# Eight experts' weights prepared beside the QKV projection, low-half stores moved to SyncE's queue, and ring registers kept for the down products

## The chip, the cores and the metric

The kernel runs on one core of a Trainium2 chip. The core has five engines with queues of their own: TensorE (PE), VectorE (DVE), ScalarE (ACT), GpSimd (POOL) and SyncE (SP). They share 16 DMA engines. A transfer is issued from the queue of one engine; in the profile those of SP are in q1 (hardware_dynamic) and those of POOL in q0 (software_dynamic). The metric is the device time of one execution in microseconds. Times differ by about 0.2% between executions of one kernel (2583.82 to 2589.56 us in three runs of the kernel before).

## The reference, cut to what matters

Two transformer layers over x of 2 x 1024 tokens of width 512, all float32. The change touches the first two of their four parts:

```
x = x + attention(layernorm(x))      # 16 heads of width 32, causal, per batch of 1024 tokens
x = x + experts(layernorm(x))        # 32 experts, top 8 per token, inner width 192
...
# attention
q, k, v = x @ Wq + bq, x @ Wk + bk, x @ Wv + bv        # per head
y = softmax(mask(q @ k.T) * scale) @ v
out = concat(y) @ Wo + bo
# experts
w, e = softmax(top_k(x @ gate_w.T, 8)), indices
h = silu(x @ w_gate[e].T) * (x @ w_up[e].T) * w
out = sum over e of h @ w_down[e].T
```

## The kernel before, in words

Matrix products are made of float32 values split in a high half (rounded to the form that PE reads fast, called fp32r in the profile) and a low half (the rest); a product is then the sum of high x high, low x high and high x low. So each operand has to be split first, and each split costs a copy for the high half and a subtraction for the low one.

**The QKV stage** (`norm_and_project`). x is 16 tiles of 128 tokens. Each is normalized by DVE, turned over by PE (`turn`), and its halves x_hi and x_lo are kept in SBUF for all tokens. The projection of queries and keys has 32 steps (`STEPS`: 4 groups of 512 tokens x 8 columns of 128 outputs), each of 12 matmuls into one of four PSUM buffers; a step for the values (`values`, 12 matmuls) follows every second of them. For every q/k step n, ACT writes the high half (`high_qk`, tile qk_hi), DVE the low half (`low_qk`, tile qk_lo), and both go to DRAM, 256 KB each, since attention wants them in another layout. There are three buffers of each (`BUFS = 3`): step n+3 waits until the stores of step n have landed. The high half is stored from SP's queue (L312), the low half from POOL's (L326). `home` gives the place of a store in DRAM: 4 heads x 32 rows x 512 tokens, so 128 rows of 2 KB.

The order on PE is written out: `UNITS` are the q/k and value steps. The turning of the 12 later tiles stands between the first 12 units, one after each.

**The attention stage** (`attend`). 16 heads, two per loop body. While PE, ACT and DVE work on a head, POOL splits expert weights that the later experts stage needs: per head two experts, each with a load of gate/up weights (768 KB), a cast and a subtraction, a store of both halves (1536 KB), then the same for the down weights (512 KB in, 768 KB out). POOL also copies each head's values into v_pair (L577), and PE's `output` waits for that. The q and k rows of the next heads are loaded by SP (L651, L655) when the columns of a head are done; the head's result is stored by SP too (L667, L668).

**The experts stage**. 160 blocks of 128 rows, 16 to a loop body on PE. Each step of PE turns the x of the next block, makes the down product of the block two steps back (`down`, L1453), turns h of the one before and makes the gate/up product of its own block (`up`, L1433). The weights lie in a ring in SBUF, and `ring_place` (L1424) loads the ring place of a block from a table into a register of PE's sequencer: once for `up` and again, two steps later, for `down` of the same block.

Each stage ends when all engines have passed it, the stores' landing included: SP waits for hi_stored and POOL for lo_stored at the end of the QKV stage.

Of the kernel before, what the change touches and what calls it, by code (L numbers as in the profile page):

```python
# [12 lines left out]
P = 128  # L13
# [212 lines left out]
def attention(nc, x_in, x_res, x_loaded, ident, w, b_qk, b_v, wo, bo, w_raw, w_split):  # L226

    qk = {n: nc.dram_tensor(f"{n}_parts", (HEADS, 2, DH, N_TOK), F32).ap() for n in "qk"}
    with ExitStack() as ctx:
        inv_sums = nc.dram_tensor("inv_sums", (HEADS, N_TOK), F32).ap()  # L230
        v_rows = ctx.enter_context(nc.sbuf_tensor("v_rows", [P, TILES, D], F32))
        yT = nc.dram_tensor("yT", (HEADS, DH, N_TOK), F32).ap()
        all_sums = nc.dram_tensor("prob_sums", (HEADS, N_TOK), F32).ap()
        norm_and_project(nc, x_in, x_res, x_loaded, ident, w, b_qk, b_v, bo, qk, v_rows)
# [6 lines left out]
def norm_and_project(nc, x_in, x_res, x_loaded, ident, w, b_qk, b_v, bo, qk, v_rows):  # L241
# [15 lines left out]
    UNITS = [unit for n in range(MT) for unit in ([("qk", n)] if n % V_EVERY < V_EVERY - 1 else [("qk", n), ("v", n // V_EVERY)])]  # L257
    assert len(UNITS) == TILES - SUB and BATCH * T == N_TOK
    with ExitStack() as ctx:
        sb = lambda n, s, dt=F32: ctx.enter_context(nc.sbuf_tensor(n, s, dt))  # L260
        x_hi, x_lo = sb("a_x_hi", [P, KD, N_TOK], F32R), sb("a_x_lo", [P, KD, N_TOK], F32R)
# [5 lines left out]
        hi, lo = sb("qk_hi", [P, BUFS, GROUP], F32R), sb("qk_lo", [P, BUFS, GROUP], F32R)  # L267
        ps_x = [ctx.enter_context(nc.psum_tensor(f"a_ps_x{b}", [P, KD, P], F32)) for b in range(2)]
# [9 lines left out]
        hi_stored, lo_stored = [sem(f"qk_hi_stored{b}") for b in range(BUFS)], [sem(f"qk_lo_stored{b}") for b in range(BUFS)]  # L278
        block = ctx.enter_context(nc.Block())
        pair = lambda p: slice(p * PAIR, (p + 1) * PAIR)  # L280
        toks = lambda i: slice(i * P, (i + 1) * P)
# [7 lines left out]
        @block.sync  # L289
        def _(sp):  # L290
            def load_w(c):
                for n in range(c * KD, (c + 1) * KD):
                    col, k = PIECES[n]
                    if n >= STAGES:
                        sp.wait_ge(w_lo_done, n - STAGES + 1)
                    sp.dma_start(stage[n % STAGES][:, :], w[k * P:(k + 1) * P, col * D:(col + 1) * D]).then_inc(w_loaded[n % STAGES], 16)

            def load_x(q):
                load_quarter(sp, x_in, x_res, q, x_loaded[q])

# [12 lines left out]
            for b in range(BUFS):  # L313
                sp.wait_ge(hi_stored[b], 16 * len(range(b, len(STEPS), BUFS)))

        @block.gpsimd
        def _(pool):
# [11 lines left out]
            for b in range(BUFS):  # L329
                pool.wait_ge(lo_stored[b], 16 * len(range(b, len(STEPS), BUFS)))  # L330

        @block.tensor
        def _(pe):
# [8 lines left out]
            def project(n):  # L342
# [10 lines left out]
                for i, (k, a, x) in enumerate(terms):  # L353
                    last = nc.tensor.matmul(ps[n % PS][:, :], a[:, k, m * P:(m + 1) * P], x[:, k, g * GROUP:(g + 1) * GROUP], start=(i == 0), stop=(i == 3 * KD - 1))
# [14 lines left out]
            for u, (kind, n) in enumerate(UNITS):  # L369
# [4 lines left out]
                turn(SUB + u)  # L374
            for n in range(MT, len(STEPS)):
                project(n)
                if n % V_EVERY == V_EVERY - 1:
                    values(n // V_EVERY)

        @block.scalar  # L380
        def _(act):
# [30 lines left out]
            for u, (kind, n) in enumerate(UNITS):  # L412
                if kind == "qk":
                    high_qk(n)
                high_x(SUB + u)
                if u % PAIR == 1 and u // PAIR + 3 < PAIRS_OF_TILES:
                    deviations(u // PAIR + 3)
                if 1 <= u <= KD:
                    high_w(2 * KD + u - 1)
            for n in range(MT, len(STEPS)):  # L420
                high_qk(n)

        @block.vector
        def _(dve):
# [46 lines left out]
            for u, (kind, n) in enumerate(UNITS):  # L471
                i = SUB + u
                if u % PAIR == 0 and u // PAIR + 3 < PAIRS_OF_TILES:
                    pair_moments(u // PAIR + 3)
                if i + 1 < TILES:
                    normalize(i + 1)
# [4 lines left out]
                low_x(i)  # L481
            dve.wait_ge(bias_o_loaded, 16)
            for n in range(MT, len(STEPS)):
                low_qk(n)
                if n - MT < TILES:
                    nc.vector.tensor_tensor(x_res[:, n - MT, :], x_res[:, n - MT, :], bias_o[:, :], ALU.add)
                if n % V_EVERY == V_EVERY - 1:
                    add_v(n // V_EVERY)


def attend(nc, qk, v_rows, yT, all_sums, w_raw, w_split, wo, wo_hi, wo_lo):
# [19 lines left out]
    FROM_POOL = 11 + E  # L511
    CONSTS = FROM_POOL + 4 + 2 * E
    assert len(ROWS) == PER_UNIT and NCH == 12 and N_LOW == 8 and EXPERTS == 2 * HEADS
    with ExitStack() as ctx:
# [30 lines left out]
        def _(pool):  # L545
# [18 lines left out]
            start = lambda it, e: isinstance(it, int) and it == 0 and e == 0  # L564

            def load_gu(p, x):
                pool.dma_start(raw_gu[x][:, :], w_raw[bass.ds(p, 1), :, :GU].rearrange("e p c -> p (e c)")).then_inc(gu_loaded[x], 16)

            def load_dn(p, x):
                pool.dma_start(raw_dn[x][:, :], w_raw[bass.ds(p, 1), :, GU:].rearrange("e p c -> p (e c)")).then_inc(dn_loaded[x], 16)  # L570

            def take_v(it, e):
                u = unit(it, e)
                if not (isinstance(it, int) and it == 0):
                    pool.wait_ge(pv_done, (u - 1) * PER_UNIT + BATCH * RING)
                    pool.sem_inc(turns_begun, 1)
                nc.gpsimd.tensor_copy(v_pair[e][:, :, :DH], v_rows[:, :, bass.ds(u * DH, DH)]).then_inc(v_ready, 1)  # L577

            def split_gate_up(it, e, x, final):
                u = unit(it, e)  # L580
                p = u * 2 + x
                hi = gu_parts[x][:, :GU]
                pool.wait_ge(gu_loaded[x], u * 16 + 16)
                pool.sem_inc(turns_begun, 1)
                if not start(it, e):
                    pool.wait_ge(gu_stored[x], u * 16)
# [7 lines left out]
                pool.dma_start(w_split[bass.ds(p, 1), :, :2 * GU].rearrange("e p c -> p (e c)"), gu_parts[x][:, :].bitcast(F32)).then_inc(gu_stored[x], 16)  # L594
                if not final:
                    load_gu(p + 2, x)

            def split_down(it, e, x, final):
                u = unit(it, e)
                p = u * 2 + x  # L600
                hi, lo, rest = dn_parts[:, :D], dn_parts[:, D:2 * D], dn_parts[:, 2 * D:]
                pool.wait_ge(dn_loaded[x], u * 16 + 16)
                pool.sem_inc(turns_begun, 1)
                if not (start(it, e) and x == 0):
# [12 lines left out]
                pool.dma_start(w_split[bass.ds(p, 1), :, 2 * GU:].rearrange("e p c -> p (e c)"), dn_parts[:, :].bitcast(F32)).then_inc(dn_stored, 16)  # L617
                if not final:
# [13 lines left out]
            with pool.Fori(1, BODIES - 1) as it:  # L632
                body(it, False)
            body(BODIES - 1, True)
# [6 lines left out]
            for x in range(2):  # L641
                pool.wait_ge(gu_stored[x], 16 * HEADS)
            pool.wait_ge(dn_stored, 16 * EXPERTS)
# [353 lines left out]
REST_W = D  # L997
W_RAW = W_GU + D + REST_W
# [337 lines left out]
def experts(nc, x_res, ident, x_rows, acc, block_meta, token_of, w_split, acc_ready, lut, idx, w_ffn, xg_all, ring, gu_loaded, dn_loaded):  # L1336
# [10 lines left out]
    with ExitStack() as ctx:  # L1347
# [64 lines left out]
        def _(pe):  # L1412
# [32 lines left out]
            def down(m, b, w, turn):  # L1445
                place = ring_place(m)
# [9 lines left out]
            def step(it, b):  # L1456
                nxt, down_of, turn_of, own = [at(it, b, d, X_TURNS if d == 1 else TURNS) for d in (1, -2, -1, 0)]
                if exists(own[0]):
                    place = ring_place(own[0])
                if exists(nxt[0]):  # L1460
                    turn_x(*nxt)
                if exists(down_of[0]):
                    down(*down_of[:2], *at(it, b, -2, U)[1:])
                if exists(turn_of[0]):
                    turn_h(*turn_of[:2])
                if exists(own[0]):
                    up(it, *own[:2], b, place)

            turn_x(0, 0, 0)
            for b in range(U):  # L1470
                step(0, b)
            with pe.Fori(1, BODIES - 1) as it:
                for b in range(U):
                    step(it, b)
            for j in range(BLOCKS - U, BLOCKS + 2):
                step(j // U, j % U)
# [1307 lines left out]
```

## Time and profile before

| | |
|---|---|
| median of three runs | 2588.65 us (2583.82 to 2589.56) |
| profiled execution | 2587.39 us, its span 2585.9 us |
| PE busy in the span | 2338.6 us (90%) |
| mean granted clock of PE | 0.945 of full speed |
| QKV stage | from the start to 174 us |
| attention stage | 174 to 633 us |
| experts stage, PE's steps | 811 to 1471 us |

Times in a profile are microseconds from the start of the span. A matmul's end is modelled, so rows overlap: the distance between two starts tells PE's pace, the length of a row does not. The share of a DMA queue is the time that its packets took, as a share of 16 engines over the window: a queue that keeps all 16 busy shows about 100%.

### The profile page before, as it was taken

How to read it: one execution, taken by the hardware profiler on the slowest of the kernel's cores; microseconds unless marked ns; L12 is line 12 of the kernel's file. 1: busy time of each engine (PE TensorE's matmuls, PEld its weight loads, DVE VectorE, ACT ScalarE, POOL GpSimd, SP SyncE). 2: the span in 40 equal slices, each digit the busy share in tenths (PEclk: the TensorE clock that was granted, in tenths of full speed). 3: DMA queues.
4: the chain of work that ended last, by engine and by line, in shares of the span. 5: the costliest groups of instructions: out<-in, count | busy, mean ns of one | idle time of the engine just before them, and what ended most of it. 6: DMA issues, size and time to landing. Idle time of an engine off the chain costs nothing. (4 is left out here: it accounts for less than half of the span.)

```text
span 2585.9 us, 48018 instructions
## 1 busy us (share of the span) xinstructions
PE 2338.6 (90%) x12710; PEld 1780.5 (69%) x12712; DVE 1505.8 (58%) x3155; ACT 979.0 (38%) x2202; POOL 1093.8 (42%) x993
## 2 busy tenths in 40 slices
PE   7969898996756999999999779999989998899998
PEld 5855454453635888988888648888856665788886
DVE  6436666663566555555555356999346665655554
ACT  3114555553254444444444342222255554311111
POOL 3128888776003665666667411111256663000000
PEclk9978999998866999999999879999999999999999
DMA  5458999996355999999999644446589761000001
GB/s 177 125 164 314 341 332 335 341 326 252 117 200 163 266 278 278 254 257 271 262 256 214 114 140 137 171 170 216 162 209 219 167 171 30 20 25 24 24 10 66
DMA packets 263308, 491.20 MB, mean 190 GB/s; under 512 B 31889, under 2 KB 149137, under 8 KB 253458
## 3 DMA queue, kind: packets, MB, share of 16 engines
q1 hardware_dynamic: 197202, 272.17, 34.3%
q0 software_dynamic: 62976, 212.42, 29.1%
q10 hardware_dynamic: 3024, 5.29, 0.6%
q8 instruction: 55, 0.90, 0.1%
q14 instruction: 51, 0.42, 0.1%
HBM read 592.96 MB, written 198.79 MB: 306 GB/s over the span
## 5 line engine op out<-in xcount | busy, mean ns | idle before, releaser
L1433 PE MATMUL m_ps_u<-m_ring,m_xT_hi 128*128 x1280 | 369.8, 350 | 0.5 <-DVE m_xT_lo L1543 0.5
L1399 POOL DMA_INDIRECT expert_sum<-x_res,token_of x160 | 256.2, 1601 | 189.4 <-DMA expert_sum<-x_res,token_of 71.1
L808 ACT ACTIVATE probs<-ps_c 128x512 f32<-128x512 f32 (+3 forms) x384 | 179.7, 491 | 208.3 <-PE ps_c L741 105.4
L1433 PEld LDWEIGHTS m_ps_u<-m_ring,m_xT_hi 128*128 128x128 f32 x1280 | 235.9, 189 | 1.2 <-issue 0.9
L709 PE MATMUL ps_r<-k_st,q_st 96*128 96x512 f32 (+3 forms) x384 | 164.6, 435 | 57.8 <-DVEq L831 22.3
L1433 PE MATMUL m_ps_u<-m_ring,m_xT_lo 128*128 x640 | 216.5, 338 | 0.0
L1392 POOL DMA_INDIRECT m_xg<-x_rows,token_of x160 | 172.6, 1078 | 100.6 <-issue 92.6
L1871 PE MATMUL s_ps<-s_x_hi,s_w_hi 128*128 128x512 f32 x512 | 199.7, 390 | 1.6 <-POOL s_w_lo L1841 1.6
L1871 PE MATMUL s_ps<-s_x_lo,s_w_hi 128*128 128x512 f32 x512 | 199.2, 389 | 0.0
L1871 PE MATMUL s_ps<-s_x_hi,s_w_lo 128*128 128x512 f32 x512 | 199.2, 389 | 0.0
L2638 DVE TENSOR_TENSOR x_res<-f_ps_o,x_res 128x512 f32<-128x512 f32 x176 | 109.3, 684 | 142.8 <-PE f_ps_o L2531 142.8
L1557 DVE SCALAR_TENSOR_TENSOR m_h<-m_silu,m_xg,m_ps_u 128x128 f32<-128x128 f32 x160 | 55.6, 348 | 233.3 <-ACT m_silu L1496 233.3
L1453 PE MATMUL m_ps_y<-m_ring,m_hT_hi 128*128 x480 | 178.1, 425 | 9.8 <-issue 8.3
L838 DVE TENSOR_REDUCE neg_max<-ps_r 128x1 f32<-128x512 f32 (+3 forms) x256 | 138.1, 584 | 62.0 <-PE ps_r L711 31.7
L1919 ACT ACTIVATE s_out<-s_ps 128x512 f32<-128x512 f32 x128 | 76.5, 599 | 254.0 <-PE s_ps L1871 254.0
L739 PE MATMUL ps_c<-q_st,k_st 128*128 128x512 f32 (+3 forms) x384 | 162.6, 428 | 0.6 <-ACT probs L808 0.5
L1839 POOL CAST s_w_hi<-s_raw 128x512 fp32r<-128x512 f32 x32 | 23.2, 726 | 308.7 <-PE s_ps L1871 215.5
L752 PE MATMUL ps_y<-probs,v_pair 128*33 128x512 f32 (+3 forms) x768 | 152.3, 521 | 0.0
L1496 ACT ACTIVATE m_silu<-m_ps_u 128x192 f32<-128x192 f32 x160 | 53.0, 331 | 235.9 <-PE m_ps_u L1433 235.9
L1502 ACT COPY x_res<-m_ps_y 128x512 f32<-128x512 f32 x160 | 94.1, 588 | 113.8 <-PE m_ps_y L1453 113.8
L709 PEld LDWEIGHTS ps_r<-k_st,q_st 96*128 96x128 f32 x384 | 83.2, 217 | 73.2 <-issue 22.9
L2251 PE MATMUL s_ps_o<-s_w_out_sb,gated 128*128 128x512 f32 x256 | 125.1, 615 | 5.7 <-DVE gated L2378 3.9
(357 smaller groups left out, 5793.7 us busy)
## 6 DMA issues: line engine op xcount, KB each, us to landing
m_ring<-w_split SPq DMA_DIRECT2D x160, 1536.0 KB
m_ring<-w_split SPq DMA_DIRECT2D x160, 768.0 KB
w_split<-e_gu_parts POOLq DMA_DIRECT2D x32, 1536.0 KB
proj<-s_out SPq DMA_DIRECT2D x32, 1024.0 KB, 3.9
e_raw_gu<-w_experts POOLq DMA_DIRECT2D x32, 768.0 KB
w_split<-e_dn_parts POOLq DMA_DIRECT2D x32, 768.0 KB
e_raw_dn<-w_experts POOLq DMA_DIRECT2D x32, 512.0 KB
q_st<-q_parts SPq DMA_DIRECT2D x32, 256.0 KB
```

The costliest lines, as they stand in the source:

```text
L709: last = nc.tensor.matmul(ps[:, :w], q_st[e][:K_QK, a, tb * P:(tb + 1) * P], k_st[e][:K_QK, a, c:c + w], start=True, stop=not diagonal)
L739: last = nc.tensor.matmul(ps[:, :width], k_st[e][:, a, s * P:(s + 1) * P], q_st[e][:, a, t0:t0 + width], start=True, stop=not diagonal)
L752: nc.tensor.matmul(ps_y[a * COL:a * COL + VW, t0 % HALF:t0 % HALF + width], v_pair[e][:, a * TB + s, :], probs[a][j % RING][:, :width], st ...
L808: nc.scalar.activation(probs[a][j % RING][:, :width], ps_c[(j * BATCH + a) % BUFS][:, :width], ACT.Exp, scale=SCALE).then_inc(exp_done, 1)
L838: nc.vector.tensor_reduce(dst, ps_r[n % BUFS][:, :w], AX.X, ALU.max, negate=True).then_inc(max_done, 1)
L1392: pool.indirect_dma_start(xg[j % X_TURNS][:, :], None, x_rows, rows_at(j), bounds_check=PADDED - 1, oob_is_err=True).then_inc(x_loaded[j % ...
L1399: pool.indirect_dma_start(acc[j % 2], rows_at(j), y[j % TURNS], None, bounds_check=PADDED - 1, oob_is_err=True, compute_op=ALU.add).then_i ...
L1433: last = nc.tensor.matmul(ps_u[b % 2][:, :W_UP], x[b % 2][:, k, :], ring[:, first + k * GU_ROW:][:, bass.ds(place, W_UP)], start=(n == 0), ...
L1453: last = nc.tensor.matmul(ps_y[b % 2][:, :], a[b % 2][:, c, :], ring[:, first:][:, bass.ds(place, D)], start=(n == 0), stop=(n == len(term ...
L1871: last = nc.tensor.matmul(ps[g][:, :], w[:, k, :], x[:, k, of_group(g)], start=(n == 0), stop=(n == 3 * KD - 1))
L2251: last = nc.tensor.matmul(ps_o[tt][:, :], gated[b][:, k, tt * P:(tt + 1) * P], w_o[:, k, :], start=(k == 0), stop=(k == KO - 1))
L2638: nc.vector.tensor_tensor(x_res[:, i, :], ps_o[s][:, :], x_res[:, i, :], ALU.add).then_inc(added, 1)
```

## The change

Four things are changed.

1. In the QKV stage, x_hi and x_lo are rings of two token groups in place of all four, and the 12 later tiles are turned over one after every third unit over the whole stage.
2. The SBUF that this frees holds buffers for expert weights. POOL splits the weights of experts 0 to 7 there, one after the other through single buffers, after the 12 pieces of the QKV weights. POOL issues no q/k stores any more: SP stores both halves.
3. In attention POOL splits the other 24 experts, 6 per body of four heads (one beside the first and third head, two beside the second and fourth).
4. In the experts stage the register of `ring_place` is kept from `up` for the `down` two steps later. Only the first two steps of a loop body load it again.

```diff
+    RING_X = 2 * GROUP
+    tile_turned = lambda u: SUB + u // PER_TURN if u % PER_TURN == 0 and SUB + u // PER_TURN < TILES else None
-        x_hi, x_lo = sb("a_x_hi", [P, KD, N_TOK], F32R), sb("a_x_lo", [P, KD, N_TOK], F32R)
+        x_hi, x_lo = sb("a_x_hi", [P, KD, RING_X], F32R), sb("a_x_lo", [P, KD, RING_X], F32R)
...
@@ norm_and_project, block.sync
             for n in range(len(STEPS)):
                 sp.wait_ge(hi_done, n + 1)
                 sp.dma_start(home(n, 0), hi[:, n % BUFS, :].bitcast(F32)).then_inc(hi_stored[n % BUFS], 16)
+                sp.wait_ge(lo_done, n + 1)
+                sp.dma_start(home(n, 1), lo[:, n % BUFS, :].bitcast(F32)).then_inc(lo_stored[n % BUFS], 16)
@@ norm_and_project, block.gpsimd
+            def split_gate_up(p):
+                hi = gu_parts[:, :GU]
+                pool.wait_ge(gu_loaded, (p + 1) * 16)
+                if p > 0:
+                    pool.wait_ge(gu_stored, p * 16)
+                nc.gpsimd.tensor_copy(hi, raw_gu[:, :]).then_inc(gu_split, 1)
+                pool.wait_ge(gu_split, p * 2 + 1)
+                nc.gpsimd.tensor_tensor(gu_parts[:, GU:], raw_gu[:, :], hi.bitcast(F32), ALU.subtract).then_inc(gu_split, 1)
+                pool.wait_ge(gu_split, p * 2 + 2)
+                pool.dma_start(w_split[p, :, :2 * GU], gu_parts[:, :].bitcast(F32)).then_inc(gu_stored, 16)
+                if p + 1 < SPLIT_EARLY:
+                    load_gu(p + 1)
...
-            for n in range(2 * KD):
+            for n in range(3 * KD):
                 split_w(n)
-            for n in range(len(STEPS)):
-                pool.wait_ge(lo_done, n + 1)
-                pool.dma_start(home(n, 1), lo[:, n % BUFS, :].bitcast(F32)).then_inc(lo_stored[n % BUFS], 16)
-                if n < KD:
-                    split_w(2 * KD + n)
+            load_gu(0)
+            load_dn(0)
+            for p in range(SPLIT_EARLY):
+                split_gate_up(p)
+                split_down(p)
@@ norm_and_project, block.tensor (block.scalar and block.vector alike)
-                turn(SUB + u)
-            for n in range(MT, len(STEPS)):
-                project(n)
-                if n % V_EVERY == V_EVERY - 1:
-                    values(n // V_EVERY)
+                if tile_turned(u) is not None:
+                    turn(tile_turned(u))
@@ attend, block.gpsimd
+    PER_TURN, HEADS_PER_TURN = 6, 4
             def body(it, final):
-                for e in range(E):
-                    take_v(it, e)
-                    for x in range(2):
-                        split_gate_up(it, e, x, final and e == E - 1)
-                        split_down(it, e, x, final and e == E - 1)
+                for h, splits in enumerate(((0,), (1, 2), (3,), (4, 5))):
+                    take_v(it, h)
+                    for n in splits:
+                        split_gate_up(it, n, final)
+                        split_down(it, n, final)
@@ experts stage, block.tensor
             def step(it, b, places):
...
                 if exists(own[0]):
-                    place = ring_place(own[0])
+                    places.append(ring_place(own[0]))
...
-                    down(*down_of[:2], *at(it, b, -2, U)[1:])
+                    down(*down_of[:2], *at(it, b, -2, U)[1:], places[-3 if exists(own[0]) else b - 2] if b >= 2 or not exists(own[0]) else ring_place(down_of[0]))
```

SP's queue in the QKV stage before, at the first q/k stores. The last three numbers are heads, rows and tokens of the place in DRAM:

```order
L309 DMA b_o_sb<-bo 128x512
L312 DMA q_parts<-qk_hi 4x32x512 x4
L312 DMA k_parts<-qk_hi 4x32x512 x4
L312 DMA q_parts<-qk_hi 4x32x512 x4
L312 DMA k_parts<-qk_hi 4x32x512 x4
```

The same place of SP's queue in the changed kernel:

```order
L320 DMA b_o_sb<-bo 128x512
L323 DMA q_parts<-qk_hi 4x32x512
L325 DMA q_parts<-qk_lo 4x32x512
L323 DMA q_parts<-qk_hi 4x32x512
L325 DMA q_parts<-qk_lo 4x32x512
L323 DMA q_parts<-qk_hi 4x32x512
L325 DMA q_parts<-qk_lo 4x32x512
```

32 stores of low halves have come to SP's queue, one behind each high half; their number and size over both queues is as before.

POOL's queue in the QKV stage before (w_qkv_lo are the low halves of the QKV weights):

```order
L320 TENSOR_TENSOR w_qkv_lo<-a_stage,w_qkv_hi 128x512 x8
L326 DMA q_parts<-qk_lo 4x32x512
L320 TENSOR_TENSOR w_qkv_lo<-a_stage,w_qkv_hi 128x512
L326 DMA q_parts<-qk_lo 4x32x512
L320 TENSOR_TENSOR w_qkv_lo<-a_stage,w_qkv_hi 128x512
L326 DMA q_parts<-qk_lo 4x32x512
```

And in the changed kernel (p_gu_parts and p_dn_parts are both halves of one expert's weights):

```order
L334 TENSOR_TENSOR w_qkv_lo<-a_stage,w_qkv_hi 128x512 x12
L337 DMA p_raw_gu<-w_experts 128x1536
L340 DMA p_raw_dn<-w_experts 128x1024
L347 CAST p_gu_parts<-p_raw_gu 128x1536
L349 TENSOR_TENSOR p_gu_parts<-p_raw_gu,p_gu_parts 128x1536
L351 DMA w_split<-p_gu_parts 128x3072
L337 DMA p_raw_gu<-w_experts 128x1536
L360 CAST p_dn_parts<-p_raw_dn 128x512
L361 CAST p_dn_parts<-p_raw_dn 128x512
L363 TENSOR_TENSOR p_dn_parts<-p_raw_dn,p_dn_parts 128x512
L365 TENSOR_TENSOR p_dn_parts<-p_raw_dn,p_dn_parts 64x512
L367 DMA w_split<-p_dn_parts 128x1536
```

The last four splits of QKV weights stand no longer between stores, and eight rounds of expert weights follow them.

PE's queue in the experts stage before, at the start of a step (m_ps_x is the turned x, m_ps_y the down product):

```order
L1424 TENSOR_LOAD block_meta_sb
L1424 ISA x2
L1420 MATMUL m_ps_x<-ident,m_xg 128x128 x4
L1424 TENSOR_LOAD block_meta_sb
L1424 ISA x2
L1453 ISA
L1453 MATMUL m_ps_y<-m_ring,m_hT_hi 128x512
L1453 MATMUL m_ps_y<-m_ring,m_hT_lo 128x512
```

The same step in the changed kernel:

```order
L1468 TENSOR_LOAD block_meta_sb
L1468 ISA x2
L1464 MATMUL m_ps_x<-ident,m_xg 128x128 x4
L1496 ISA
L1496 MATMUL m_ps_y<-m_ring,m_hT_hi 128x512
L1496 MATMUL m_ps_y<-m_ring,m_hT_lo 128x512
```

The second load of a register and what goes with it are gone from in front of the down product, in 14 of 16 steps.

## Rows read from the trace of the kernel before

**Rows 1.** The page: busy time by engine.

```profile
PE 2338.6 (90%) x12710; PEld 1780.5 (69%) x12712; DVE 1505.8 (58%) x3155; ACT 979.0 (38%) x2202; POOL 1093.8 (42%) x993
```

**Rows 2.** Windows (length, busy us of each engine, PEclk, DMA share, GB/s): QKV, attention.

```profile
60.00:160.00 100.00, 100.00 (x447) 82.81 (x446) 37.97 (x57) 17.59 (x26) 16.89 (x25) 1.00 0.46 122
185.00:626.00 441.00, 403.88 (x2172) 221.11 (x2172) 274.55 (x495) 223.48 (x463) 356.49 (x337) 0.92 0.92 330
```

**Rows 3.** DMA queues, 60 to 160 us: packets, MB, share of 16 engines.

```profile
q0 software_dynamic: 6411, 6.10, 25.9%
q1 hardware_dynamic: 3042, 6.04, 19.9%
```

**Rows 4.** DMA queues, 96 to 106 us.

```profile
q1 hardware_dynamic: 438, 0.87, 24.4%
```

**Rows 5.** DMA queues, 104 to 105 us.

```profile
q1 hardware_dynamic: 47, 0.09, 26.1%
```

**Rows 6.** DMA queues, 709 to 710 us (256 KB stores x_rows<-m_ln_xn, rows of 2 KB).

```profile
q1 hardware_dynamic: 206, 0.37, 96.3%
```

**Rows 7.** Timeline of SP: first q/k stores, and the first load of attention.

```profile
26.63 14.17 SPq L312 DMA_DIRECT2D q_parts<-qk_hi  x4
...
174.38 1.37 SPq L651 DMA_DIRECT2D q_st<-q_parts  x2
```

**Rows 8.** Windows at the end of the QKV stage.

```profile
172.00:174.00 2.00, 0.00 (x0) 0.00 (x0) 0.00 (x0) 0.00 (x0) 0.00 (x0) 0.50 0.02 6
```

**Rows 9.** Timeline of PE: q/k matmuls at half clock and at full clock.

```profile
21.34 0.63 PE L354 MATMUL qk_ps<-a_x_lo,w_qkv_hi 128*128 128x512 f32 x1
21.77 0.63 PE L354 MATMUL qk_ps<-a_x_hi,w_qkv_hi 128*128 128x512 f32 x1
...
100.15 0.39 PE L354 MATMUL qk_ps<-a_x_hi,w_qkv_hi 128*128 128x512 f32 x1
100.38 0.39 PE L354 MATMUL qk_ps<-a_x_hi,w_qkv_lo 128*128 128x512 f32 x1
```

**Rows 10.** DMA queues and issues, 210 to 600 us.

```profile
q0 software_dynamic: 16266, 104.31, 71.1%
w_split<-e_gu_parts POOLq DMA_DIRECT2D x29, 1536.0 KB
```

**Rows 11.** Timeline of POOL: v_pair of two heads, two experts between them.

```profile
325.55 0.61 POOL L577 COPY v_pair<-v_rows 128x512 f32 x1
...
352.75 0.61 POOL L577 COPY v_pair<-v_rows 128x512 f32 x1
```

**Rows 12.** Waits of PE, 185 to 626 us: us in total, times, longest.

```profile
PE ps_r L709 <- DMA q_st<-q_parts: 21.9, 11, 3.0
PE ps_r L709 <- DVE neg_max L838: 13.1, 11, 3.3
```

**Rows 13.** Windows of one head each: the first of eight, and their sum.

```profile
299.30:326.86 27.56, 24.57 (x144) 13.13 (x145) 18.31 (x33) 15.69 (x33) 22.19 (x22) 1.00 0.94 329
...
sum 220.50, PE 200.31 PEld 109.44 DVE 143.62 ACT 115.07 POOL 178.56; mean PE 25.04 PEld 13.68 DVE 17.95 ACT 14.38 POOL 22.32
```

**Rows 14.** Timeline of DVE and of POOL at 341 us.

```profile
341.47 2.80 DVE L850 CAST max_cols<-neg_max 128x8 fp32r<-128x8 f32 x1
...
340.80 3.44 POOL L591 TENSOR_TENSOR e_gu_parts<-e_raw_gu,e_gu_parts 128x1536 fp32r<-128x1536 f32 x1 [0.18 <-POOL e_gu_parts L588]
```

**Rows 15.** Waits of PE, 820 to 1475 us.

```profile
PE m_ps_y L1453 <- issue: 8.3, 22, 1.0
```

**Rows 16.** Line L1424: count, duration ns min/median/max, first and last start.

```profile
L1424 PEldq TENSOR_LOAD <-block_meta_sb x320: 295/304/1180, 810.7 to 1467.4; - x160
```

**Rows 17.** Timeline of PE: first down matmul of three successive steps.

```profile
1258.72 0.48 PE L1453 MATMUL m_ps_y<-m_ring,m_hT_hi 128*128 x1
...
1262.65 0.49 PE L1453 MATMUL m_ps_y<-m_ring,m_hT_hi 128*128 x1
...
1267.03 0.49 PE L1453 MATMUL m_ps_y<-m_ring,m_hT_hi 128*128 x1 [0.18 <-issue]
```

More of the change, by code:

```diff
@@ L256, in norm_and_project @@
     PIECES = [(c, k) for c in (0, 2, 1) for k in range(KD)]
-    UNITS = [unit for n in range(MT) for unit in ([("qk", n)] if n % V_EVERY < V_EVERY - 1 else [("qk", n), ("v", n // V_EVERY)])]
-    assert len(UNITS) == TILES - SUB and BATCH * T == N_TOK
+    UNITS = [unit for n in range(len(STEPS)) for unit in ([("qk", n)] if n % V_EVERY < V_EVERY - 1 else [("qk", n), ("v", n // V_EVERY)])]
+    PER_TURN = len(UNITS) // TILES
+    RING_X = 2 * GROUP
+    GU, DN = W_GU, W_RAW - W_GU
+    assert PER_TURN * TILES == len(UNITS) and BATCH * T == N_TOK
+    tile_turned = lambda u: SUB + u // PER_TURN if u % PER_TURN == 0 and SUB + u // PER_TURN < TILES else None
+    tile_normalized = lambda u: tile_turned(u + 2)
+    pair_begun = lambda u: tile_turned(u + 4) // PAIR if tile_turned(u + 4) is not None and tile_turned(u + 4) % PAIR == 0 and u > 0 else None
     with ExitStack() as ctx:
         sb = lambda n, s, dt=F32: ctx.enter_context(nc.sbuf_tensor(n, s, dt))
-        x_hi, x_lo = sb("a_x_hi", [P, KD, N_TOK], F32R), sb("a_x_lo", [P, KD, N_TOK], F32R)
+        x_hi, x_lo = sb("a_x_hi", [P, KD, RING_X], F32R), sb("a_x_lo", [P, KD, RING_X], F32R)
         w_hi, w_lo = sb("w_qkv_hi", [P, KD, 3 * D], F32R), sb("w_qkv_lo", [P, KD, 3 * D], F32R)
@@ L353, in project @@
                 for i, (k, a, x) in enumerate(terms):
-                    last = nc.tensor.matmul(ps[n % PS][:, :], a[:, k, m * P:(m + 1) * P], x[:, k, g * GROUP:(g + 1) * GROUP], start=(i == 0), stop=(i == 3 * KD - 1))
+                    last = nc.tensor.matmul(ps[n % PS][:, :], a[:, k, m * P:(m + 1) * P], x[:, k, group_toks(g)], start=(i == 0), stop=(i == 3 * KD - 1))
                 last.then_inc(product, 1)
@@ L414, in _ @@
                     high_qk(n)
-                high_x(SUB + u)
-                if u % PAIR == 1 and u // PAIR + 3 < PAIRS_OF_TILES:
-                    deviations(u // PAIR + 3)
+                if tile_turned(u) is not None:
+                    high_x(tile_turned(u))
+                if pair_begun(u) is not None:
+                    deviations(pair_begun(u))
                 if 1 <= u <= KD:
                     high_w(2 * KD + u - 1)
-            for n in range(MT, len(STEPS)):
-                high_qk(n)
         @block.vector
@@ L471, in _ @@
             for u, (kind, n) in enumerate(UNITS):
[L472 to L476, printed above, removed]
+                if pair_begun(u) is not None:
+                    pair_moments(pair_begun(u))
+                if tile_normalized(u) is not None and u > 0:
+                    normalize(tile_normalized(u))
                 if kind == "qk":
@@ L480, in _ @@
                     add_v(n)
[L481 to L488, printed above, removed]
+                if tile_turned(u) is not None:
+                    low_x(tile_turned(u))
+                if u == len(UNITS) - TILES:
+                    dve.wait_ge(bias_o_loaded, 16)
+                if u >= len(UNITS) - TILES:
+                    t = u - (len(UNITS) - TILES)
+                    nc.vector.tensor_tensor(x_res[:, t, :], x_res[:, t, :], bias_o[:, :], ALU.add)
 def attend(nc, qk, v_rows, yT, all_sums, w_raw, w_split, wo, wo_hi, wo_lo):
@@ L511, in attend @@
     FROM_POOL = 11 + E
+    PER_TURN, HEADS_PER_TURN = 6, 4
+    TURNS = HEADS // HEADS_PER_TURN
     CONSTS = FROM_POOL + 4 + 2 * E
-    assert len(ROWS) == PER_UNIT and NCH == 12 and N_LOW == 8 and EXPERTS == 2 * HEADS
+    assert len(ROWS) == PER_UNIT and NCH == 12 and N_LOW == 8 and EXPERTS - SPLIT_EARLY == PER_TURN * TURNS
     with ExitStack() as ctx:
@@ L631, in _ @@
             body(0, False)
-            with pool.Fori(1, BODIES - 1) as it:
+            with pool.Fori(1, TURNS - 1) as it:
                 body(it, False)
-            body(BODIES - 1, True)
+            body(TURNS - 1, True)
             pool.wait_ge(wo_loaded, 16)
@@ L997 @@
 REST_W = D
+SPLIT_EARLY = 8
 W_RAW = W_GU + D + REST_W
@@ L1443, in turn_h, with down @@
                 last.then_inc(h_turned, 1)
-            def down(m, b, w, turn):
-                place = ring_place(m)
+            def down(m, b, w, turn, place):
                 pe.wait_ge(dn_loaded[w], turn * 16 + 16)
@@ L1466, in step @@
                 if exists(own[0]):
-                    up(it, *own[:2], b, place)
+                    up(it, *own[:2], b, places[-1])
             turn_x(0, 0, 0)
+            places = []
             for b in range(U):
-                step(0, b)
+                step(0, b, places)
             with pe.Fori(1, BODIES - 1) as it:
+                places = []
                 for b in range(U):
-                    step(it, b)
+                    step(it, b, places)
+            places = []
             for j in range(BLOCKS - U, BLOCKS + 2):
-                step(j // U, j % U)
+                step(j // U, j % U, places)
         @block.scalar
```

83 lines of the change are left out of this document (53 added, 30 removed).

## The prediction, on record before the changed kernel ran

> **What bounds the kernel now.** I read the page first: PE is busy for 90% of the span [rows 1], so only a stage in which PE waits has anything to give. The windows by stage come next. In the QKV stage PE is busy for all of 60 to 160 us, POOL for 17 us and the DMA engines for 46% [rows 2]: PE bounds it, and POOL and DMA look free. In attention POOL is busy for 356 of 441 us, DMA for 92%, PE for 404 us at a mean granted clock of 0.92 [rows 2]. The waits tell what PE lacks there: 21.9 us for q_st loads, 13.1 us for DVE's maxima [rows 12]. In the experts stage PE's only listed wait of size is 8.3 us of "issue" ahead of the down product [rows 15].
>
> Then the DMA view of the QKV stage, queue by queue, because the change puts two kinds of traffic there. q1, SP's queue, carries only the high-half stores and has a share of 19.9% over 100 us [rows 3]. In 10 us when it is pressed it has 24.4%, and in one full microsecond 26.1% with 47 packets [rows 4, 5]. The same queue with stores of the same size and row length has 96.3% and 206 packets in a microsecond elsewhere [rows 6]. A share of a quarter that holds level under pressure is 4 engines of 16. What differs is the place in DRAM: 4 heads x 32 rows x 512 tokens, as the order shows, against plain rows. So SP's q/k stores run on four engines, and these are nearly full already: 19.9 of 25.
>
> By the Trainium skill (DMA: Bandwidth & Descriptors, "Why a DMA increments its semaphore by 16 and not by 1") a DMA runs on the largest number of engines up to 16 that divides the slowest dimension of both sides, here 4, and on SP's queue on the lowest-numbered ones, always the same. By that rule the low halves, once on SP's queue, join the high ones on the same four engines; the trace agrees on the number (24.4%).
>
> **The change, part by part.**
>
> *The stores.* A store is 128 rows of 2 KB. At 47 to 48 packets a microsecond it takes 128/48 = 2.67 us of the four engines [rows 5]. Before, q1 had one such store per q/k step, and PE needs 18 matmuls at 0.227 us (12 and half a value step) = 4.1 us for a step [rows 9]: hidden. Now q1 has two, 5.33 us a step, which is more than PE's 4.1. With three buffers a half, up to six stores queue, 16 us of work, so the four engines never run dry; ACT's and DVE's next halves wait for landings and PE for its PSUM buffers. 64 stores x 2.67 = 171 us, from the first at 26.6 us [rows 7]. Bounds: the same 2.67 us from below (the best microsecond), and from above the mean over 60 to 160 us, 0.199 x 1600/3042 = 0.105 us a packet, x 32 = 3.35 us a store, 214 us in all [rows 3]. That mean holds time lost to the other queue, which I count below, so I take 2.67.
>
> *The experts' traffic there.* In 390 us of attention q0 had 71.1% for 29 experts: 0.711 x 390/29 = 9.56 us of all 16 engines, so of each of the four too [rows 10]. Eight experts: 76.5 us. A store waits for the slowest engine it uses, so this adds to the 171 us if the packets of both queues take turns. Bounds: 0 (the queues overlap wholly) to 76.5; the mean packet of q1 grows from 0.089 us [rows 4] to 0.105 [rows 3] where q0 is busier, so they take turns; I take 76.5. Data then end at 26.6 + 171 + 76.5 = 274 us. Before, they ended at 172 us [rows 8]. The stage grows by **102 us**; from the bounds by 26.6 + 171 - 172 = 26 to 26.6 + 214 + 76.5 - 172 = 145 us.
>
> *POOL's own eight rounds* take 27.2/2 = 13.6 us each with double buffers [rows 11]; with single ones and a loaded ring I take 16, at most 20. From about 45 us, when the twelfth weight piece is split, that is 128 us (160 at most), ending at 173 (205) us: beside the stores, worth nothing while those last till 274. If they didn't, it would be the late one by some 3 us. The twelve turns spread over the stage move 48 transposes and no work; their cover is the same, and the waits for them before the first 12 units are at most a few us. The ring of two groups adds no wait: group g+2 is turned over after the first unit of group g+1, when group g has been read.
>
> *The bias additions* (16 on DVE) have two SBUF inputs. In attention a cast of 8 columns took 2.80 us and ended with POOL's subtraction of 3.44 us that had begun before it [rows 14]. At worst each addition waits 3.44 us, 55 us of DVE time, against 62 of 100 us that DVE is idle [rows 2]; and by then POOL is through. Nothing. The Trainium skill has the rule (SBUF — State Buffer: the pair of ports that DVE and GpSimd share is an exclusive lock, taken by a DVE operation with two SBUF inputs or in a two-port mode); the trace agrees with 2.80 us.
>
> *Attention.* POOL has 24 experts for 98 us per four heads at PE's pace: 6 x 13.6 + 4 x 0.6 = 84 us. It stops being level with PE (27.2 us a head against 27.56) [rows 11, 13]. What can go is PE's waits, 21.9 + 13.1 = 35 us [rows 12], and the clock that falls behind them: 1 - 0.92 of 441 us is 35 us at most, of which the start and the end, without this cause, have some 15, so 20 [rows 2]. Upper bound 55 us; lower bound 0, since every load and store left is one that was there. What is late next is the same q_st load wherever a pair of experts runs over a head's end: after POOL's double rounds, two heads in four. So I take half, **25 us** less.
>
> *The registers.* 14 of 16 steps lose a register load of 0.30 us and its two instructions ahead of the down product. From below, 8.3 us of issue waits x 14/16 = 7 us [rows 15]. From above, 160 steps in 656.6 us are 4.10 us each [rows 16] against 3.93 in a step without delay [rows 17]: 0.17 x 160 x 14/16 = 24 us. The delayed step of 4.38 us lists only 0.18 of wait [rows 17], so the truth is over the lower end, but the load for `up` stays and delays too. I take **13 us** less.
>
> *Sum*, against the profiled execution (2587.39 us, span 2585.9): +102 - 25 - 13 = +64, 2651 us; it lay 1.3 us under the median of the runs, so 2652.7, rounded **2652 us**. Its own range, with attention 0 to 55, registers 7 to 24 and packets slightly better or worse packed, is 2620 to 2680.
>
> **The rivals.**
>
> *A: the low stores don't share the four engines* (another set is taken for each store, or all 16). Then q1 could carry both, PE stays the bound until 163 us, and the stage ends with POOL's eighth expert, 3 to 30 us later, say 10. Time 2588.65 + 10 - 25 - 13 = 2561 us. For it: DMA is at 46% on average [rows 2], so there is room if it is spread. Against: 24.4% level over 10 us with two stores issued. 10%. Faster.
>
> *B: the queues overlap on an engine*, so that the experts' packets cost the stores nothing: +26 - 38 = 2577 us. Against: the longer packets above. 5%. Faster.
>
> *C: PE at half clock sets the pace.* With PE waiting for a quarter of each step and more, its granted clock may stay at 1.2 GHz. A step is then 18 x 0.43 = 7.7 us [rows 9], 32 of them 246 us from 20 us on: 266 us, no later than the stores alone with the experts. Only where it adds up, in the last 90 us after the experts, does it cost, some 15 us: 2667 us. For it: PE was at half clock at 21 us after idling. Against: four PSUM and three SBUF buffers let PE work in long runs. 10%.
>
> *D: everything at its bad end*: stores at 3.35 us, attention no better, 2588.65 + 145 - 13 = 2721 us. 5%.
>
> **How the numbers follow.** Forecast 70%, A 10%, B 5%, C 10%, D 5%. A change of less than 0.2%, 5 us, can't be told from none. Faster 0.15 (A, B), same 0.01, slower 0.84. The range leaves out A, B and D: 2600 to 2690, wider at the low end for experts' packets that cost the stores only a part.
>
> **What would show it.** QKV stage: SP's first q_st load near 277 us in place of 174; q1 with a share near 25% whenever q0 is idle, through to the end of the stage, 47 to 48 packets a microsecond at most; ACT and DVE waiting for DMA, PE for qk_lo, its clock partly 0.5; POOL idle after some 175 us. Attention: heads of about 26 us, alternating shorter and longer, q_st waits halved. Experts: nearly all steps at 3.95 us. The prediction is wrong if q1 shows over 30% in that stage (A), if the stage ends before 240 us (B), or if its end is POOL's.

## The result, and the profile after

The changed kernel takes 2642.85 us (median of 4 runs, 2637.79 to 2652.3), the kernel before 2588.22 us (4 runs): a ratio of 1.0214, 95% interval 1.0196 to 1.0232, slower by some 55 us. The forecast was 2652 us. The profiled execution of the changed kernel is its longest run, 2652.3 us with a span of 2650.8 us; its experts' stage is looked at below.

I divide the span at SP's first load of q_st, its first load of o_sums (the end of attention) and TensorE's first and last register load in the experts' stage ("loads"). A kernel that keeps its registers has no load for its last two down products, so its last load comes some 6 us earlier for this reason alone; the column "down" goes from the first to the last down matmul and is without this fault. Lengths in us, each from one trace:

```
                        to first q_st   attention   loads     down     span
before                      174.4         459.2     656.7     647.9   2585.9
after                       267.0         431.4     652.1     650.0   2650.8
```

The page's busy times of after, which answer to [rows 1]:

```profile
PE 2336.0 (88%) x12710; PEld 1783.8 (67%) x12712; DVE 1486.2 (56%) x3155; ACT 977.7 (37%) x2202; POOL 1070.8 (40%) x961
```

Windows of after (length, busy us of PE, PEld, DVE, ACT, POOL, granted clock, DMA share, GB/s): two of the QKV stage and one of attention, which ends with the last matmuls of attention as the one before does; the answer to [rows 2].

```profile
60.00:160.00 100.00, 53.28 (x204) 42.21 (x202) 20.50 (x34) 9.64 (x17) 64.36 (x59) 0.78 0.71 267
160.00:267.00 107.00, 60.24 (x252) 48.89 (x252) 32.04 (x53) 11.96 (x19) 10.79 (x11) 0.79 0.34 131
278.00:693.00 415.00, 395.63 (x2168) 216.16 (x2170) 257.40 (x495) 222.39 (x462) 274.73 (x257) 0.94 0.80 280
```

TensorE has as much to do as before and is now busy for half of the time: 53 microseconds of 100 where there were 100. From 160 us on the DMA engines move only 131 GB/s, so the stage is waiting for DMA while they are busy for a third of the time. The queues show it. After, 60 to 160 us (packets, MB, share of 16 engines; to [rows 3]):

```profile
q0 software_dynamic: 3389, 21.60, 58.0%
q1 hardware_dynamic: 2540, 5.04, 13.0%
```

After, 200 to 260 us, with the experts done (all packets, then q1; to [rows 4]), and the microsecond from 223 us (to [rows 5]):

```profile
DMA packets 3089, 6.16 MB, mean 103 GB/s; under 512 B 93, under 2 KB 93, under 8 KB 3087
q1 hardware_dynamic: 3087, 6.13, 26.3%
...
q1 hardware_dynamic: 52, 0.10, 26.8%
```

Alone, q1 sits at a quarter of the engines without a gap: 3087/60 = 51.4 packets a microsecond. 93 of them are under 512 bytes, four beside the 128 rows of each store, so a store is 132 packets and takes 2.57 us; 6.13 MB in 60 us, 102 GB/s, say the same. Over the stretch with q0 it gets half of that. SP's timeline after, to [rows 7] (start, duration):

```profile
25.58 0.75 SPq L323 DMA_DIRECT2D q_parts<-qk_hi  x1
26.38 0.56 SPq L325 DMA_DIRECT2D q_parts<-qk_lo  x1
...
266.98 1.37 SPq L694 DMA_DIRECT2D q_st<-q_parts  x2
```

Waits after, up to 267 us (total, times, longest):

```profile
POOL causal_mask L592 <- POOLq L42: 90.5, 1, 90.5
DVE qk_lo L500 <- DMA k_parts<-qk_lo: 87.8, 13, 11.6
...
PE a_ps_x L388 <- DVE a_ln_xn L489: 66.6, 8, 13.1
...
DVE qk_lo L500 <- DMA q_parts<-qk_lo: 62.4, 14, 12.4
...
POOL p_gu_parts L347 <- DMA p_raw_gu<-w_experts: 43.3, 8, 7.1
...
ACT qk_hi L446 <- DMA k_parts<-qk_hi: 35.1, 7, 9.1
ACT qk_hi L446 <- DMA q_parts<-qk_hi: 33.8, 7, 11.3
...
PEld qk_ps L403 <- DVE qk_lo L500: 15.0, 3, 10.1
```

ACT and DVE wait for stores to land, 219 us between them. POOL is through with its eight experts at 176 us and stands idle for 90.5. TensorE waits for DVE, but mostly for a_ln_xn: on DVE the normalization of the next token tile stands behind a low_qk that waits for its slot, and so the transposes are in most cases late before a PSUM buffer is. A PSUM buffer is what it waits for in three places (qk_lo, 15.0 us, listed at the weight loads).

Attention after: PE's waits from 278 to 707 us (to [rows 12]) and q0 from 300 to 690 us (to [rows 10]).

```profile
PE ps_r L752 <- DVE neg_max L881: 9.2, 8, 3.7
PE ps_r L752 <- DMA q_st<-q_parts: 8.9, 6, 2.2
```

```profile
q0 software_dynamic: 12825, 82.33, 55.7%
```

35 us of waits are 18, PE's busy time is 396 us where it was 404 [rows 2], and POOL now waits for PE at v_pair (76.6 us in 7 waits) where it was level with it [rows 11]. In the experts' stage PE's "issue" wait at the down product is 5.5 us where it was 8.3 [rows 15], and the register loads are 178 where they were 320 [rows 16]:

```profile
PE m_ps_y L1496 <- issue: 5.5, 9, 1.2
```

```profile
L1468 PEldq TENSOR_LOAD <-block_meta_sb x178: 295/304/1344, 875.7 to 1527.8; - x178
```

### The profile page after: what moved, and what is told of

It is laid out like the page before. It is cut to its first block and busy times, and to the rows that moved or that the text cites. A ratio compares the mean times of both kernels' runs of the same rounds, so it can differ in the third digit from the quotient of the medians.

```text
span 2650.8 us, 47347 instructions
## 1 busy us (share of the span) xinstructions
PE 2336.0 (88%) x12710; PEld 1783.8 (67%) x12712; DVE 1486.2 (56%) x3155; ACT 977.7 (37%) x2202; POOL 1070.8 (40%) x961
```

## The experiments

Eight kernels. The same division of each trace, with the medians of the runs:

```
                               first q_st  attention  loads     down    median us (runs)  ratio to before, 95%
before                            174.4      459.2     656.7    647.9    2588 to 2590
after                             267.0      431.4     652.1    650.0    2642.85 (4)       1.0214 [1.0196, 1.0232]
stores by head (e1)               200.7      427.5     642.1    640.1    2575.2 (10)       0.9937 [0.9914, 0.996]
stores by pair of heads (e2)      430.4      425.0     644.3    642.3    2802.84 (1)
low stores from ACT (e3)          267.4      429.3     637.1    634.9    2639.66 (1)
before, low stores on SP (e5)     197.2      462.0     657.9    649.9    2614.47 (4)       1.0091 [1.0063, 1.0118]
before, registers kept (e6)       171.9      458.8     640.2    638.8    2574.99 (11)      0.9959 [0.9937, 0.9982]
after, part outermost (e7)        174.0      431.7     652.5    651.1    2564.44 (4)       0.991  [0.9883, 0.9936]
before, part outermost (e8)       166.1      463.1     663.2    654.4    2580.8 (10)       0.9974 [0.9953, 0.9995]
after, 32 rounds in attention (e9) 265.8     457.3     643.3    641.3    2675.46 (1)
```

Kernels with (1) were executed once, so no interval is given for them.

**e1: each store as four transfers, one a head** (HT is 4 heads, P is 128 rows; the low stores and the counts of the semaphores likewise).

```
+    SPLIT = 4
...
-                sp.dma_start(home(n, 0), hi[:, n % BUFS, :].bitcast(F32)).then_inc(hi_stored[n % BUFS], 16)
+                for q in range(SPLIT):
+                    sp.dma_start(home(n, 0)[q * HT // SPLIT:(q + 1) * HT // SPLIT], hi[q * P // SPLIT:(q + 1) * P // SPLIT, n % BUFS, :].bitcast(F32)).then_inc(hi_stored[n % BUFS], 16)
```

> The changed kernel with each q/k store on SP's queue issued as four transfers, one per head (32 rows of 2 KB each), so 256 transfers in place of 64, same bytes, same queue. Theory 'four engines': 32 rows can be spread over 16 engines, a step's two stores then cost under 2 us of all engines, PE or POOL bounds the stage again. Attention's first q_st load at about 180 us in place of 267, q1's share in the QKV stage over 30% in some microseconds, time 2643 - 87 = about 2556 us (2545 to 2570). Rival 'the queue itself carries no more than 100 GB/s of such stores': nothing changes, first q_st load at 267 us or later (four times the issues), time 2643 us or more.

Measured 2575.2 us: faster than before, but 20 us over the expected value, with the first q_st load at 200.7. Queues of this run, 60 to 160 us, then 175 to 195 us, and SP's timeline in the second stretch:

```profile
q0 software_dynamic: 3746, 23.32, 64.9%
q1 hardware_dynamic: 6342, 8.67, 27.8%
```

```profile
q1 hardware_dynamic: 2044, 2.81, 55.6%
```

```profile
186.80 1.84 SPq L325 DMA_DIRECT2D k_parts<-qk_hi  x4
188.69 1.84 SPq L328 DMA_DIRECT2D k_parts<-qk_lo  x4
190.57 1.83 SPq L325 DMA_DIRECT2D k_parts<-qk_hi  x4
```

q1 passes 25%: a transfer from one head isn't bound to four engines. What holds the end now is SP, which issues without a gap: four transfers of 64 KB take 1.88 us from one group to the next, 139 GB/s, which is the 141 that q1 moves. The engines' work from 26.6 to 200 us comes to some 141 us of all sixteen, so over the whole stage they were not the floor, though from 60 to 160 us they were busy for 93%.

**e2: two transfers of two heads each** (the same edit with `SPLIT = 2`).

> The changed kernel with each q/k store issued as two transfers of two heads each (2 x 32 rows x 512 tokens). Theory 'the number of engines is set by the slowest dimension of the place in DRAM': now two engines carry all stores, 64 packets each per store, so 64 x 5.0 = 320 us, plus the experts' packets on those two engines, 78 us: the stage's data end near 27 + 320 + 78 = 425 us, first q_st load near 428 us, q1 at 12.5 to 13% and 50 GB/s when alone, time 2643 + 161 = about 2804 us. Rival 'each transfer has a fixed small number of engines, or the queue has a rate of its own': 267 us and 2643 us as in the changed kernel, or less.

Measured 2802.84 us. 300 to 400 us:

```profile
q1 hardware_dynamic: 2573, 5.11, 13.1%
```

```profile
430.45 0.64 SPq L697 DMA_DIRECT2D q_st<-q_parts  x1
```

The same bytes, the same 2 KB rows, twice the transfers, and half the rate. One head, two heads and four heads give over 50%, 13% and 26%: neither the queue nor the length of a row sets the rate, the outermost count of the transfer does. The Trainium skill (DMA: Bandwidth & Descriptors, "Why a DMA increments its semaphore by 16 and not by 1") says that a DMA takes the largest number of engines up to 16 that divides the slowest dimension of both sides; for 2 that is 2 engines, an eighth, and the trace agrees with 13.1%; for one head, whose slowest dimension is its 32 rows, it is all 16, and the trace agrees in that e1 passes 50%.

**e3: the low stores issued by ACT,** one step late, behind the next high half; SP keeps the high ones.

```
+            def store_low(n):
+                act.wait_ge(lo_done, n + 1)
+                act.dma_start(home(n, 1), lo[:, n % BUFS, :].bitcast(F32)).then_inc(lo_stored[n % BUFS], 16)
```

> The changed kernel with the low halves stored from ACT's queue (one step late, after the next high half is computed) in place of SP's; the high halves stay on SP's. Theory 'the same four engines whatever the hardware queue': the two queues share the four engines, the stage ends as late as in the changed kernel, first q_st load 262 to 270 us, both queues together at 25 to 26% when POOL's queue is idle, time 2640 to 2650 us. Rival 'a queue is limited, not the engines': the two queues together reach twice the rate, first q_st load at about 180 to 200 us, time about 2560 to 2575 us.

Measured 2639.66 us. 200 to 250 us:

```profile
q1 hardware_dynamic: 1287, 2.55, 13.1%
q10 hardware_dynamic: 1286, 2.55, 13.1%
```

A second hardware queue adds nothing: together 51.5 packets a microsecond, the rate of q1 alone. So both use the same four engines. Before, the low stores went through POOL's software queue, and that was not so: q0's 25.9% and q1's 19.9% [rows 3] are more than four engines have.

**e5: the kernel before with the low stores on SP.** POOL's stores go, and its last four pieces of the QKV weights follow the others at once.

```
+                sp.wait_ge(lo_done, n + 1)
+                sp.dma_start(home(n, 1), lo[:, n % BUFS, :].bitcast(F32)).then_inc(lo_stored[n % BUFS], 16)
...
```

> The kernel before with one edit: the low halves' stores are issued by SP behind the high ones, not by POOL (no expert weights in the QKV stage, all 32 in attention, registers as before). Theory: stores alone take 64 x 2.49 us (the pace that the changed kernel shows when nothing else moves, 26.3% share) = 159 us from 26.6 on, first q_st load at 26.6 + 159 + 3 = 189 us in place of 174.4, so +15 us; with the 2.67 us of the prediction 200 us and +26. Time 2588 + 15 = 2603 us (2600 to 2615). Rival 'the slowdown is the experts' traffic alone': no change, 2588 us.

Measured 2614.47 us; first q_st load at 197.21, eight microseconds later than expected, five of them because a store takes 2.57 us and not 2.49. 60 to 160 us:

```profile
q1 hardware_dynamic: 5139, 10.21, 26.3%
```

The stores' move alone costs 197.2 - 174.4 = 22.8 us in this stage. The remaining 267.0 - 197.2 = 69.8 us I put down to the experts' packets on the same engines. It is a difference, since no run adds the experts alone: after has the ring of two groups and the spread turns as well. Against these as a cause, the GB/s of after from 60 to 100 us, one number a microsecond, fall in every pause of q0 to q1's own pace, 98 to 104, and not below it, and so they go on to the end (96 at the least up to 180 us, then q1 at 25 to 26% alone). So from 60 us on q1 did not lack stores. And e7 has the ring and the turns too, and no loss.

```profile
GB/s 358 371 408 416 227 160 117 102 98 100 104 408 412 418 299 227 348 383 397 406 397 201 125 98 104 98 104 174 385 408 412 289 238 313 389 412 406 383 176 131
```

**e6: the kernel before with the registers kept**, the part of the change in `down` and `step` alone.

> The kernel before with the last part of the change alone (the ring places of the down products kept in registers). My theory prices it at 13 us, all in the experts' stage: 2576 us (2569 to 2582), and the stage from the first to the last register load on TensorE 644 us long instead of 657. The rival: the reads are hidden behind other work and the changed kernel's profile, with a stage only 4.6 us shorter, tells what they are worth: 2584 us or more.

Measured 2574.99 us, by the medians -13.3 us; by the ratio -10.6, with an interval from -4.7 to -16.3. Line L1424 of this run, and its down matmuls beside those of before:

```profile
L1424 PEldq TENSOR_LOAD <-block_meta_sb x178: 296/306/1417, 808.0 to 1448.2; - x178
...
L1452 PE MATMUL m_ps_y<-m_ring,m_hT_hi x480: 387/396/503, 818.3 to 1457.1; 128*128 x160
```

```profile
L1453 PE MATMUL m_ps_y<-m_ring,m_hT_hi x480: 387/396/503, 821.9 to 1469.8; 128*128 x160
```

The first to the last load is 640.2 us against 656.7 [rows 16], but the last load of before belongs to the last down product and that of e6 to a product two steps earlier. Between the same two matmuls it is 638.8 us against 647.9: -9.1. PE's "issue" wait at the down product is 9.5 us in this run, not less than before's 8.3, so that row doesn't tell the gain. The rival (nothing gained) falls.

**e7: the changed kernel with the part outermost in q_parts and k_parts.** A store is then 128 plain rows; attention loads q and k by twelve transfers a head in place of eight.

```
-    qk = {n: nc.dram_tensor(f"{n}_parts", (HEADS, 2, DH, N_TOK), F32).ap() for n in "qk"}
+    qk = {n: nc.dram_tensor(f"{n}_parts", (2, HEADS, DH, N_TOK), F32).ap() for n in "qk"}
-            return qk[...][h0:h0 + HT, part, :, g * GROUP:(g + 1) * GROUP]
+            return qk[...][part, h0:h0 + HT, :, g * GROUP:(g + 1) * GROUP].rearrange("h d t -> (h d) t")
```

> The changed kernel with q_parts and k_parts laid out with the part outermost, so that a store is 128 rows of 2 KB in one transfer. My theory: all sixteen engines carry a store again and SyncE issues two transfers a step instead of the eight of the run by heads; the stage goes back to near TensorE's own time or the sum of the transfers (the run by heads had 141 us of full engines from 26.6 us on): first q_st load at 180 us (174 to 190), total 2555 us (2545 to 2570). The rival, that the sum of experts' and stores' bytes bounds the stage however it is issued, gives the run by heads again: first load near 200, 2575 us. Attention loads q and k by twelve transfers a head instead of eight; I count that as nothing, and if it costs, the stretch of attention is longer than 427 us.

Measured 2564.44 us, the best of all: 0.991 of before, and inside the range expected. Its windows:

```profile
60.00:100.00 40.00, 40.00 (x187) 33.09 (x185) 23.76 (x38) 9.49 (x17) 29.34 (x27) 1.00 1.00 357
100.00:140.00 40.00, 40.00 (x184) 33.09 (x183) 24.27 (x32) 7.98 (x14) 25.84 (x24) 1.00 0.95 347
```

```profile
q0 software_dynamic: 2883, 18.37, 61.9%
q1 hardware_dynamic: 5338, 9.72, 35.0%
```

TensorE is busy without a gap at full clock, and DMA is full beside it (the second fence is 60 to 140 us). The loss of the stage, 93 us, is gone with one change of layout, and the rival (the sum of the bytes) falls. POOL is now last: its last store is issued at 166.50, after SP's at 157.66.

```profile
166.50 0.56 POOL L367 DMA_DIRECT2D w_split<-p_dn_parts  x1 [0.30 <-POOL p_dn_parts L365]
173.91 0.20 POOL L592 MEMSET causal_mask<- 128x128 bf16 x1 [6.85 <-POOLq L42]
```

**e8: the kernel before with the same layout.**

> The kernel before with the same layout alone. Its projections were paced by TensorE and its stores shared between two queues, so my theory expects no change: 2588 us (2580 to 2597), first q_st load at 174. If the four engines had held the kernel before back as well, it is faster; if twelve loads a head cost attention something, it is slower, and the stretch of attention says by how much.

Measured 2580.8 us, 0.9974 with an interval just short of 1: a small gain, 7.5 us by the medians, where I had expected none. The first q_st load is at 166.1 in place of 174.4, and SP's last store of the stage is issued by 158.6, not at 162.9. So the four engines cost the kernel before some 4 us of TensorE's pace and 4 us at the end. Twelve loads a head cost attention at most a few microseconds: 463.1 here and 431.7 in e7 are each the longest of their kind, 3.9 and 2.4 us over the median. On this layout the change is worth 2564.44 - 2580.8 = -16 us; the rest of e7's -24 is the layout's own gain.

**e9: the changed kernel with all 32 experts prepared in attention** (the function `attend` of the kernel before; the first eight are prepared twice).

> The changed kernel's first stage with the attention of the kernel before, which prepares all 32 experts again (the first eight twice). If the 28 us that attention gained come from the rounds taken out of it, attention is 459 us long again, the first q_st load stays at 267, and the total is 2670 us (2662 to 2680). If attention was faster for another reason (the later start, other loads), it stays near 431 and the total near 2643.

Measured 2675.46 us. 278 to 719 us:

```profile
278.00:719.00 441.00, 400.55 (x2170) 217.74 (x2169) 265.94 (x495) 224.14 (x463) 358.18 (x335) 0.93 0.92 330
```

Attention is 457.3 us long again and the first stage stays at 265.8: the gain comes from the eight rounds taken out of it, not from its later start.

## Why the prediction was right, step by step

*That SP's store runs on four engines, and that two of them a step outlast TensorE:* right, shown by e1, e2 and e7, which change nothing but how a store is cut or laid out (in e7 also how it is read back) and move the first q_st load from 267 to 201, 430 and 174.

*The stores' term, 171 us from 26.6 us:* its sum was nearly right, its unit was not, and that they meet is partly luck. I took 47 packets a microsecond and 128 a store, 2.67 us; the queue alone moves 51.4, a store has 132, and it took 2.57 us, so 64 are 164 us. In e5 the stage ended at 197.2, where the forecast has its last data at 26.6 + 171 = 197.6. The 6 us between 26.6 + 164 and 197.2 are the start, in which the queue was not full, the last landing and the change of block, which I had not counted.

*The experts' term, 76.5 us:* 69.8 as the difference of after and e5. q0's share in after adds up to 0.278 x 33.4 + 0.58 x 100 + some 12 from 160 to 180 us = 79 us of each engine, as priced, so 9 us of it cost the stores nothing. By 60 us q1 is 330 packets behind that of e5, 6.4 us of its pace, for 9.3 us of q0's traffic; the rest of the 9 us lies later. What hid them no run shows. This is the larger part of the error in the stage: +92.6 us against +102.

*POOL's rounds:* 16 us forecast, 17.1 measured (its first cast at 47.4, the second expert's at 64.5), since its loads waited on a full DMA (43.3 us at L347). It ended at 176 and cost nothing, as argued. In e7, where the stores no longer hide it, it costs 174 - 166 = 8 us against e8, more than the 3 that I gave it there and less than the 10 of rival A.

*What waits:* ACT and DVE for DMA, as forecast. PE's wait was for the most part named wrongly: I said qk_lo, which is there with 15.0 us, and it was a_ln_xn (66.6 us, 52.3 of them after 20 us) and a_x_lo (15.5), which queue behind low_qk on DVE. The price is the same, because the stores set the pace. The order on DVE costs nothing by itself: in e7, which has it too, TensorE is busy for all of 60 to 140 us.

*Attention, -25 us:* measured -27.8 in the pair. Over all traces the five with 32 rounds lie at 457.3 to 463.1 (median 459.2), the five with 24 at 425.0 to 431.7 (median 429.3): -30. The guess of half was a little low. Its two parts came nearly as priced: the waits went from 35 to 18 us and PE's busy time from 404 to 396 us, with the granted clock at 0.94 where it was 0.92. The heads do alternate, as said: from one q_st turned over (ps_turned, L763) to the next it is 25.7 and 30.7 us at the start, then 22.9 to 23.2 in one and 26.4 to 28.7 in the next.

*Registers, -13 us:* e6 has -13.3 by the medians and -10.6 by the ratio, and -9.1 between its down products. The pair of traces seems to show -4.6, but on the column "down" after is 2.1 us longer than before. Between down products most steps of after are on the forecast's mark:

```profile
1101.19 0.48 PE L1496 MATMUL m_ps_y<-m_ring,m_hT_hi 128*128 x1
...
1105.10 0.47 PE L1496 MATMUL m_ps_y<-m_ring,m_hT_hi 128*128 x1
...
1109.03 0.48 PE L1496 MATMUL m_ps_y<-m_ring,m_hT_hi 128*128 x1
```

The median step is 3.93 us (3.97 before) and the upper quartile 3.95 (4.10), but three steps take 6.3, 7.8 and 9.8 us, and PE waits 8.3 us for m_ring loads. e7 has the same (steps of 6.9, 9.4 and 11.0, waits of 10.2), in an execution of 2562.25 us, which is under its kernel's median; in e3 and e6 the longest step is 5.5 and 5.4 us and no such wait is listed. What delays a few m_ring loads in some executions I have not tried. On "down" the median of the seven traces with registers kept is 641.3 us, of the three without 649.9: -8.6. So the term was right in sign and between 9 and 13 us in size. My upper bound was somewhat high: between down products a step of before takes 4.07 us in the mean, not 4.10.

*Sum:* +92.6 - 29.9 - 8.6 = +54.1 us from these medians against +54.6 measured. That they meet this closely is luck, since single traces of a stage differ by 10 us and more. The forecast had +102 - 25 - 13 = +64: the stage 9 us too long, attention 5 us too little gained, the registers up to 4 us too much.

*The rivals:* A (the low stores don't share the four engines) falls with the 26.3% of after and e5; e7 is near the kernel that it described, at 2564 us for its 2561, though by another sum: its stage ends as early as before's and not 10 us later. B (the queues overlap on an engine) falls with the 69.8 us. C (half clock sets the pace): the granted clock was 0.78 and 0.79 in the two windows of the stage, so part of it ran at 1.2 GHz, but TensorE was idle for 47 us in each of them and from 60 us on q1 did not lack stores; the clock followed the waits and cost nothing here. D falls with 2.57 us a store.

## What to carry to other kernels

Before a transfer is moved to another queue, read the share of its queue in a stretch where that queue alone is busy: a share that stays level at 26% or 13% is a transfer confined to 4 or 2 of 16 engines, and the mean DMA share of the stage, 46% before the change, hides it. Look then at the order of the dimensions in DRAM; with the part outside the heads the same change was worth -16 us (e7 against e8) where it had been worth +55. Where a trace of one pair of executions disagrees with a priced term by ten microseconds, lay the same stage side by side in several traces before the term is given up, and measure it between two instructions that both kernels have.

## What the runs showed of the hardware that I had not expected

Splitting a transfer can halve its rate: 256 KB as one transfer over four heads went at 102 GB/s (q1, 60 to 160 us of e5), as two over two heads at 51 GB/s (e2), as four of one head at 141 GB/s (e1), there limited by SP's 0.46 us for each (1.84 us for four). And two hardware queues, of SP and of ACT, had together the rate of one: 1287 and 1286 packets in 50 us, against 3087 in 60 us of q1 alone.
